# A two-layer graph network: spherical numbers copied over rows by DMA, both layers of the weight network in plain fp32

## What is computed

```python
x_e = x[dst_of_layer]                      # node features gathered per edge
wk = relu(ea @ k_w1 + k_b1) @ k_w2 + k_b2  # per-edge weights, 64 -> 64 -> 128; wv alike
k = wk * sum_s sh[:, s] * (x_e @ Cqk[:, s, :])   # nine spherical numbers s; v alike with Cv
attn = sum over 16 of q[node] * k, 8 heads; softmax over the edges of a node
out = x @ W_self + (sum of alpha * v over the edges of a node) @ W_out
```

## Time and profile before

| | before |
|---|---|
| median of 3 runs | 2949.27 us (2947.16 to 2950.45) |
| the profiled execution | 2947.53 us |
| its span, first to last instruction | 2945.7 us |
| TensorE, VectorE busy | 2469.1 us (84%), 2612.7 us (89%) |
| ScalarE, GpSimd busy | 1514.6 us (51%), 1731.3 us (59%) |
| mean granted TensorE clock | 0.899 |
| mean DMA rate over the span | 141 GB/s |

### The profile page before, as it was taken

How to read it: one execution, slowest core, us unless ns; L and a number is a source line. 1 busy time by engine, 2 the same in 40 slices (tenths; PEclk the granted TensorE clock), 3 DMA queues, 4 the chain that set the end, 5 groups by cost and what they waited for, 6 DMA issues and landing times.

```text
span 2945.7 us, 48186 instructions
## 1 busy us (share of the span) xinstructions
PE 2469.1 (84%) x12310; PEld 1787.3 (61%) x12505; DVE 2612.7 (89%) x3389; ACT 1514.6 (51%) x2914; POOL 1731.3 (59%) x1719
## 2 busy tenths in 40 slices
PE   2233347999999999999999999999999999999714
PEld 1233315677777776777677776777677777777511
DVE  6688835899999999999999999999999999999737
ACT  1321224566666655666566665666566566666310
POOL 1800037777777766667676666666666677665030
PEclk7555557999999999999999999999999999999855
DMA  6787714245555544444444444444445544544340
GB/s 187 202 222 187 210 25 111 76 131 149 148 149 145 148 147 139 141 142 148 139 144 142 146 147 140 140 144 147 142 141 147 148 141 142 148 144 132 121 124 11
DMA packets 282407, 415.35 MB, mean 141 GB/s; under 512 B 64463, under 2 KB 191875, under 8 KB 278470
## 3 DMA queue, kind: packets, MB, share of 16 engines
q1 hardware_dynamic: 222278, 296.67, 32.4%
q0 software_dynamic: 52704, 107.19, 15.1%
q10 hardware_dynamic: 7128, 8.13, 0.8%
HBM read 309.59 MB, written 102.20 MB: 140 GB/s over the span
## 4 chain that ended last, share of the span: by engine, by line
PE 52%; DVE 7%; issue 6%; ACT 3%; DMA 2%; POOL 2%; SPq 0%; DVEq 0%; ACTq 0%; POOLq 0%
PE bank L1118 11%; PE bank L1120 9%; PE bank L1119 9%; PE bank L1142 5%; PE bank L1163 4%; PE bank L1194 2%; PE bank L1124 2%; PE bank L1125 2%; PE bank L1095 2%; PE bank L1113 2%; DVE xa_t L1538 1%; DVE z_l L1546 1%; PE bank L1102 1%; POOL gathered L745 1%; PE bank L1101 1%
## 5 line engine op out<-in xcount | busy, mean ns | idle before, releaser
L745 POOL DMA_INDIRECT gathered<-xtab_d,src_g x784 | 780.6, 996 | 449.7 <-PE bank L1095 203.0
L745 POOL DMA_INDIRECT gathered<-qtab_d,dst_g x784 | 801.9, 1023 | 257.2 <-issue 249.0
L1118 PE MATMUL bank<-z_h,wt_h 128*128 128x512 f32 x1568 | 729.6, 465 | 27.9 <-DVE val L1578 27.9
L1538 DVE TENSOR_TENSOR xa_t<-bank,r_r 128x512 f32<-128x512 f32 x980 | 667.3, 683 | 13.5 <-PE bank L1142 10.3
L876 ACT ACTIVATE z_h<-xa_t 128x512 fp32r<-128x512 f32 x980 | 617.4, 634 | 110.1 <-DVE xa_t L1538 100.3
L1120 PE MATMUL bank<-z_h,wt_l 128*128 128x512 f32 x1568 | 620.7, 396 | 0.0
L1119 PE MATMUL bank<-z_l,wt_h 128*128 128x512 f32 x1568 | 618.8, 395 | 0.0
L1546 DVE TENSOR_TENSOR z_l<-xa_t,z_h 128x1024 fp32r<-128x1024 f32 x392 | 478.0, 1219 | 48.2 <-ACT z_h L876 44.6
L1118 PEld LDWEIGHTS bank<-z_h,wt_h 128*128 128x128 f32 x1568 | 301.1, 192 | 131.4 <-issue 92.7
L869 ACT ACTIVATE hid<-bank,b1kv 128x512 f32<-128x512 f32 x196 | 134.8, 688 | 476.4 <-PE bank L1102 462.4
L1120 PEld LDWEIGHTS bank<-z_h,wt_l 128*128 128x128 f32 x1568 | 294.9, 188 | 69.2
(11 more groups left out here) (222 smaller groups left out, 4057.9 us busy)
## 6 DMA issues: line engine op xcount, KB each, us to landing
nrow_d<-x_r SPq DMA_DIRECT2D x196, 288.0 KB
ea<-in_ea_t SPq DMA_DIRECT2D x392, 128.0 KB
exb<-exd_d SPq DMA_DIRECT2D x392, 128.0 KB
dmb<-exd_d SPq DMA_DIRECT2D x392, 128.0 KB
ea_c<-in_ea_t SPq DMA_DIRECT2D x49, 512.0 KB, 5.0
aggrow_d<-xa_t SPq DMA_DIRECT2D x49, 512.0 KB, 3.9
gathered<-xtab_d,src_g POOLq DMA_INDIRECT x784
gathered<-qtab_d,dst_g POOLq DMA_INDIRECT x784
```

The lines of the kernel that those rows point to most:

```text
L745: rows_in = pool.indirect_dma_start(rows[:, c % 4, k, :], None, table, bass.IndirectOffsetOnAxis(ap=picked[:, s, at:at + 1], axis=0))
L1118: pe.matmul(ps[:, :], wt_h[rows, w, :], high, start=start, stop=False)
L1538: dve.tensor_tensor(z[:, i, :], bank[2 + (NJ * c + i) % 2][:, :], xt[:, c % 2, :], ALU.mult).then_inc(z_ok, 1)
```

## The change

1. The spherical numbers are not split or spread any more. A new `load_harmonics` on the SyncE queue copies them as fp32 from DRAM straight into a tile `sh_b` of 128 rows by five chunks: five DMAs per group, where chunk i reads two rows of the table and repeats each over 64 partitions (the last chunk reads one row and repeats it over 128). It stands first in the body, for group c + 2, and waits until the products `z` of group c are done. `sh_b` holds two groups.
2. `outer` reads `sh_b` instead of PSUM, as two instructions over 2 and 3 chunks, and `outer_high` follows with two. `OUTER` and `NZ = 2` name the cut.
3. The selector, `s3`, `sh3_d`, the splitting in setup and all its waits go.
4. `hidden` and `weights` are plain fp32 over halves of 256 edges. The edge features of the first half stand on rows 0 to 63 and those of the second on rows 64 to 127, so an edge load is half as long. `edge_high`, `edge_low` and `hidden_low` go. `hidden` moves to body c for group c + 2, writes PSUM banks 2 and 3, and `front_h` is one relu per half, placed after `batch_turned`.
5. `key_query` moves behind the batch work, `exb` moves into free room, and addresses are formed from a view by turns of 28 groups (`columns`).

```diff
+OUTER = [slice(0, 2), slice(2, NJ)]
+NZ = len(OUTER)
...
-        sel = sb("sel", [P, NJ, P], BF16)
-        s3 = sb("s3", [P, 4, G], BF16)
+        w1kv = sb("w1kv", [P, O])
+        w2kv = sb("w2kv", [P, O])
...
+        ea2 = sb("ea2", [P, 2, HG])
+        sh_b = sb("sh_b", [P, 2, NJ, G])
...
             def load_edge(j, c):
-                past(sp, eal_ok, j, c, 2)
+                past(sp, hid_ps, j, c, 2, 2)
                 hold()
                 for half in range(2):
-                    sp.dma_start(ea2[half * D:(half + 1) * D, c % 2, :], edges_t[:, bass.ds(group(j, c) * G, G)]
-                                 ).then_inc(ea_in[c % 2], 16)
...
+                    sp.dma_start(ea2[half * D:(half + 1) * D, c % 2, :],
+                                 columns(edges_t, j, c)[:, half * HG:(half + 1) * HG]).then_inc(ea_in[c % 2], 16)
+
+            def load_harmonics(j, c):
+                past(sp, z_ok, j, c, 2, NZ)
                 hold()
+                for i in range(NJ):
+                    k = 2 * i
+                    rows = columns(harmonics_t[k:min(k + 2, S), :], j, c)
+                    n = min(2, S - k)
+                    sp.dma_start(sh_b[:, c % 2, i, :], rows.rearrange("s (o w) -> s o w", o=1)
+                                 .to_broadcast([n, P // n, G])).then_inc(sh_b_in[c % 2], 16)
...
             def body(j, c):
+                if live(j, c + 2):
+                    load_harmonics(j, c + 2)
                 if live(j, c + 3):
                     load_edge(j, c + 3)
...
-            act.wait_ge(sh_in, 16)
-            for part in range(3):
...
-            def edge_high(j, c):
...
             def front_h(j, c):
-                done(act, hid_ps, j, c)
+                done(act, hid_ps, j, c, 2)
+                past(act, wk_ps, j, c, 1)
                 past(act, wv_ps, j, c, 1)
-                act.activation(hid[:, :], ps_hw[:, :], ACT.Relu, bias=b1kv[:, :]).then_inc(hid_ok, 1)
-                act.activation(hid_h[:, :], ps_hw[:, :], ACT.Relu, bias=b1kv[:, :]).then_inc(hid_ok, 1)
+                for f in range(2):
+                    act.activation(hid[:, f * HG:(f + 1) * HG], bank[2 + f][:, 0:HG], ACT.Relu, bias=b1kv[:, :]
+                                   ).then_inc(hid_ok, 1)
...
             def hidden(j, c):
...
+                for f in range(2):
+                    half = slice(f * D, (f + 1) * D)
+                    pe.matmul(bank[2 + f][:, 0:HG], w1kv[half, :], ea2[half, c % 2, :], start=True, stop=True
+                              ).then_inc(hid_ps, 1)
...
-            def spread(j, c, i):
...
+                for f in range(2):
+                    edges = slice(f * HG, (f + 1) * HG)
+                    mk = pe.matmul(ps_xw[:, edges], w2kv[0:D, :], hid[0:D, edges], start=True, stop=True)
+                    mv = pe.matmul(ps_hw[:, edges], w2kv[D:P, :], hid[D:P, edges], start=True, stop=True)
+                mk.then_inc(wk_ps, 1)
+                mv.then_inc(wv_ps, 1)
...
             def outer(j, c, i):
 
-                done(dve, shb_ps, j, c, NJ, i + 1 - NJ)
                 if i == 0:
                     done(dve, xt_ok, j, c)
                     past(dve, acc_ps, j, c, 2)
-                dve.tensor_tensor(z[:, i, :], bank[2 + (NJ * c + i) % 2][:, :], xt[:, c % 2, :], ALU.mult
-                                  ).then_inc(z_ok, 1)
+                    past(dve, zl_ok, j, c, 1, NLOW)
+                    landed(dve, sh_b_in, j, c, 16 * NJ)
+                n = OUTER[i].stop - OUTER[i].start
+                dve.tensor_tensor(z[:, OUTER[i], :], sh_b[:, c % 2, OUTER[i], :],
+                                  xt[:, c % 2, :].rearrange("p (o g) -> p o g", o=1).to_broadcast([P, n, G]),
+                                  ALU.mult).then_inc(z_ok, 1)
```

More of the change, by code:

```diff
@@ L27 @@
 NJ = 5
[L28 to L29 removed]
+CK, CV, CEND = 0, NJ, 2 * NJ
+NW = CEND
+OUTER = [slice(0, 2), slice(2, NJ)]
+NZ = len(OUTER)
 H = 8
@@ L350, in gnn_two_layers @@
         qg_in = [sem(f"qg_in{i}") for i in range(2)]
-        eah_ok = sem("eah_ok")
-        eal_ok = sem("eal_ok")
+        sh_b_in = [sem(f"sh_b_in{i}") for i in range(2)]
         batch_in = sem("batch_in")
@@ L1127, in weights @@
             def weights(j, c):
-                done(pe, hidl_ok, j, c)
+                done(pe, hid_ok, j, c, 2)
+                past(pe, wv_ok, j, c, 1)
                 if isinstance(j, int) and c + 1 >= NG:
@@ L1132, in weights @@
                     done(pe, xt_ok, j, c + 1)
-                for ps, rows, done_ps in ((ps_xw, slice(0, D), wk_ps), (ps_hw, slice(D, P), wv_ps)):
-                    split_matmul(ps, W2KV, hid_h[rows, :], hid_l[rows, :], True, True, rows).then_inc(done_ps, 1)
-            def spread(j, c, i):
-                if i == 0:
-                    landed(pe, s3_in, j, c)
-                if not isinstance(j, int) or c * NJ + i >= 2:
-                    done(pe, z_ok, j, c, NJ, i - 1 - NJ)
-                pe.matmul(bank[2 + (NJ * c + i) % 2][:, :], sel[:, i, :], s3[:, c % 4, :], start=True, stop=True
-                          ).then_inc(shb_ps, 1)
+                for f in range(2):
[4 more added lines that the diff above has]
+                mv.then_inc(wv_ps, 1)
             def products(j, c, i):
@@ L1211, in body @@
                         products(j, c, i)
-                    if i + 2 < NJ and live(j, c + 1):
-                        spread(j, c + 1, i + 2)
                     if i == 1 and live(j, c + 1):
                         weights(j, c + 1)
+                    if i == 1 and live(j, c + 2):
+                        hidden(j, c + 2)
                     s = batch_at(c, 10)
@@ L1367, in _ @@
             dve.wait_ge(wtl_ok, 1)
-            for w in (CK + 4, CV + 4, W1KV):
+            for w in (CK + 4, CV + 4):
                 dve.memset(wt_l[D:P, w, :].bitcast(F32), 0.0).then_inc(wtl_padded, 1)
@@ L1628, in body @@
                     outer(j, c + 1, 1)
-                    hidden_low(j, c + 1)
+                    outer_low(j, c + 1, 0)
                 if live(j, c - LAG):
                     sum_values(j, c - LAG)
-                if live(j, c + 1):
-                    outer_low(j, c + 1, 0)
-                    outer(j, c + 1, 2)
-                    key_query(j, c + 1)
-                    outer(j, c + 1, 3)
                 s = batch_at(c, 8)
@@ L1643, in body @@
                 if live(j, c + 1):
-                    outer(j, c + 1, 4)
+                    key_query(j, c + 1)
                     outer_low(j, c + 1, 1)
@@ L1648, in body @@
                     batch_decays(j, s)
-                if live(j, c + 2):
-                    edge_low(j, c + 2)
                 if live(j, c + 1):
```

119 lines of the change are left out of this document (28 added, 91 removed).

## The result

The changed kernel takes 6132.69 us (median of 4 runs, 6131.46 to 6134.73) beside 2949.32 us (4 runs, 2947.16 to 2950.45): a ratio of 2.080, 95% interval 2.076 to 2.083. The forecast was 6055 us in a range of 5300 to 6900. The profiled execution took 6134.73 us, its span is 6132.9.

The account below looks back on a forecast made before the run. Compute bounded the kernel before (11.74 us per group); after the change two DMA engines would, at 28.0 us. 412 + 5488 - 42 + 193 + 1.8 = 6053, so 6055 us, range 5300 to 6900.

Parts of the forecast that it names:

- Two outer rows, two engines: Main loop: the four copies of two DRAM rows run on the same two DMA engines, 524,288 B each per group; 83%.
- 21.9 + 6.1 = 28.0 us per group: Load of the two engines per group: copies 21.9 us at 23.9 KB per us, the rest of their transfers some 6.
- The sum: Whole kernel: 412 before the copies, 5488 for 196 groups, less 42, plus 193 tail and 1.8 outside the span: 6053 us.
- the discount of the first: Main loop: the first twelve groups have no exponents and row stores, so 3.5 us less each, 42 us in all.
- Setup saves 30 us, bounds 15 and 37: Setup: splitting of the spherical numbers leaves, saving 30 us; two subtractions of 7.6 us sure, 37 if an early store comes sooner.
- SyncE issues twelve transfers in some 7.5 us and waits for `z`: Main loop, per group: twelve transfers instead of eight at 0.62 us each still fit; the order of waits costs nothing.
- TensorE at a lower clock does not matter: Main loop: at the 1.2 GHz level TensorE's 10 us per group become about 20, still under 28.
- the signs: What the profile should show: groups of about 28 us, DMA share near 0.3, VectorE and TensorE busy 9 to 10 us.
- VectorE 9.6 us per group, ScalarE and GpSimd unchanged: Main loop: VectorE falls from 11.3 to 9.6 us per group; GpSimd's gathers stay about 10.7; ScalarE loses little and hides.
- All sixteen engines give 2714 us: Rival, 7%: all sixteen DMA engines share the copies, 7.4 us per group, and the change is faster at 2714 us.
- GpSimd's 10.7 us bound the group: Main loop, if sixteen engines share the copies: issuing eight gathers plus the index copy, 10.7 us, sets the group, for 11.74 before.
- fp32 layers: no change: TensorE, weight layers: six plain fp32 products, at most 3.1 us per group, replace eight split ones, at most 3.1; no change taken.

Follow-up runs that it names:

- nine copies: The changed kernel with each two-row copy cut into two copies of one row, repeated over 64 partitions: 3135.73 us, ratio 1.066 to the kernel before.
- operand in PSUM: The changed kernel with one-row copies, the turned source values kept in their own PSUM bank, first fp32 layer as one 512-column product: 2982.44 us, ratio 1.012.
- three larger transfers: The one-row-copy kernel with its eight 64-partition copies made two transfers of four chunks, three copies per group in all: 3316.38 us, ratio 1.126.

## Why the prediction was right, point by point

*Two outer rows, two engines*: right, and now shown by one edit that keeps the bytes (28.27 us at two, 17.79 at four, 13.28 at eight, 13.05 at sixteen).

*21.9 + 6.1 = 28.0 us per group*: 28.24 measured. The copies went somewhat faster than 23.9 KB per us (20.9 us at the rate of 25.0) and the rest is more (7.3). The mechanism was right; that the sum came so near is luck, two misses in size that cancel.

*The sum*: the copies begin at 402.6 us, not 412; from there to the first product of the last group it is 5537.7 us for 5446; the tail is 192.6 for 193. Together 82 us more than 6053, and the profiled execution took 6134.7. The first product of the thirteenth group starts at 737.9 us, so the first twelve groups take 25.35 us each and the others 28.43: the discount of the first was right (3.1 for 3.5 us), and the term that was too small is the full group, 0.43 us or 84 us in all.

*Setup saves 30 us, bounds 15 and 37*: 43.8 measured, outside the bounds. The term that was mis-sized is the early store to `keep_d`. The two subtractions and their waits gave what I had, 30.1 us (from the first to the fourth scan 16.45 us for 46.60). But the issue of that store fell from 14.18 to 1.67 us and the first scan came 17.0 us sooner (45.81 for 62.85), where my high end allowed 7; some 3 us were lost again later.

*SyncE issues twelve transfers in some 7.5 us and waits for `z`*: wrong in kind. It is held in the issue itself, 16 to 20 us for five copies; the prediction named this as a possibility only. What stands behind it comes late, but the two engines have work all the time, so no cost of it shows.

*TensorE at a lower clock does not matter*: right. Granted 0.70 in the mean, between its two levels of 1.2 and 2.4 GHz, and it is busy 446 / 35.4 = 12.6 us per group; I had 20 at the low level throughout, and 9 to 10 in the signs. With nine copies, at 0.95 of its clock, it is still 0.859 x 13.05 = 11.2 us, so my 10 was somewhat low.

*VectorE 9.6 us per group, ScalarE and GpSimd unchanged*: VectorE's 345 / 35.4 = 9.8 us. The gathers at 0.95 us were even cheaper than before: of the 281 from 1000 to 2000 us none starts with 0.13 us or more of a two-operand VectorE instruction left. At 28 us per group the hold does not show.

*All sixteen engines give 2714 us* (7%): the condition was rightly found not to hold, but its price was wrong. With sixteen engines it is 3136 us and slower than before. "GpSimd's 10.7 us bound the group" took the issue cost of the old VectorE code; under two-operand products of 1.2 and 1.75 us it is 13.0. And with the hold smaller the transfers came in at 12.2 to 12.3 us per group, with the engines busy at 0.90 (operand in PSUM): 11.0 us of work in each, where I had 7.4. The rate per engine was the mis-sized term. With all sixteen at work each moves 231 / (16 x 0.90) = 16.0 KB per us while busy (all traffic taken together), against 25 when two work alone; the earlier trace rows, with 16.5 on 13.6 engines, was the nearer row. Why it falls stays open. Even one-row copies together with the operand in PSUM stay 1.2% above the kernel before. The chance of faster should have been smaller still.

*fp32 layers: no change*: right for the form of the change, 1.5 us per group for 1.6 at full clock. As one product of 512 columns the first layer alone is 0.4 us dearer.

No version that computes everything beat the kernel before. Not tried: a third buffer for the copies, and copies issued from two queues. Open: how much of the slower packets of three larger transfers is their shape.

## What to carry to other kernels

Before a DMA is priced by its bytes, look at its outermost count: the same 131 KB to 64 partitions cost 28, 18 or 13 us per group when the 64 repeats were written with 2, 4 or 8 and more outermost, and the mean DMA share (0.31) gave no hint. When VectorE instructions are merged into longer ones with both operands in SBUF, count what GpSimd issues meanwhile: the merge saved VectorE 0.4 us a group and cost GpSimd 1.3 (eight gathers at 1.30 us for 1.14). A rate per DMA engine read where few engines work is too high for all of them together: 25 KB per us with two, 16 with sixteen. And when a first bound is lifted, price every next one with the new code's own instructions, not the old one's.

## What the runs showed of the hardware that was not expected

A gather's issue on GpSimd, 0.94 us, is held until the end of the two-operand VectorE instruction it starts under: 1.0 us more under one of 1.75 us in the rows shown; with both operands in SBUF but products of 0.68 us the mean rose by 0.03 us only. SyncE's issue of a copy grew from 0.6 us (5.15 us for eight, with the operand in PSUM) to 3.3 to 3.9 us while the two engines that the copies need are behind. Where only these two work they move 25 KB per us each, and 16.0 each where all sixteen are 0.90 busy. The packets of that queue took 0.105 us in the mean with transfers that go round four rows of DRAM, 0.076 us with one-row transfers, and 0.088 us with one-row transfers and fuller engines.
